# A conditional MLP with layer norm on one core: bias rows and two residual tiles ahead of the second x, GpSimd's last weight pairs over two batches, the last tile in halves

## The chip, the cores and the metric

The kernel runs on one core of a Trainium2 chip. The metric is the device time of one execution in microseconds (us), the median of the runs shown; lower is better. A core has TensorE (PE, matrix products), VectorE (DVE), ScalarE (ACT), GpSimd (POOL) and SyncE (SP), which here issues nearly all DMAs. Each engine runs its own instruction stream in order, and they wait for each other through semaphores.

## The reference

`x` is 16 batches of 512 rows by 512 columns, all fp32. An integer per batch picks one of three networks, whose output is added to `x`; the sum is normalized per row:

```python
out_nr  = gelu(x @ w1_nr  + b1_nr)  @ w2_nr  + b2_nr
out_tsr = gelu(x @ w1_tsr + b1_tsr) @ w2_tsr + b2_tsr
out_sr  = gelu(gelu(x @ w1_sr + b1_sr) @ w2_sr + b2_sr) @ w3_sr + b3_sr   # hidden 1024
out = where(c == 0, out_nr, where(c == 1, out_tsr, where(c == 2, out_sr, 0)))
y = x + out
return (y - mean(y)) * rsqrt(var(y) + 1e-5) * gamma + beta
```

## The kernel before

**Arithmetic.** Each fp32 operand is split in two parts of type fp32r, a high one and the rest (`w_hi`/`w_lo`, `x_hi`/`x_lo`, `g_hi`/`g_lo`), and a product is three matmuls: hi·hi, hi·lo, lo·hi. An NR or TSR batch is 96 matmuls of 128x512 (48 for layer 1, 48 for the last layer), an SR batch is 240. In these inputs batch 0 is NR, batch 1 is SR, batches 2 to 6 are NR. Weights are loaded once and stay in SBUF; they are split at the start: DVE and ACT split the NR weights, POOL all others, in pairs of chunks (`split_hi`, then `split_lo`; 128x1024 each). SR's pairs carry the semaphores `s_split["sr1"]`, `["sr2"]`, `["sr3"]`, TSR's four pairs `["tsr"]`.

**One batch.** PE makes the hidden layer in PSUM banks; ACT applies gelu twice per chunk (`g_hi`, and the full value in the bank); DVE makes `g_lo`; PE's last layer puts four row tiles of 128x512 in banks 4 to 7. Meanwhile SP loads the residual rows of `x` in `y`, and POOL adds the last layer's bias row to each tile (`add_bias`, semaphore `s_xb`). DVE adds the tile to the bank (`residual`), takes mean and variance (`stats`, `moments`), two tiles at a time, and makes `(y - mean) * gamma` (`centre`). POOL makes the reciprocal deviations (`deviations`, `rstd`), ACT scales by them, POOL adds beta (`shift`), SP stores the tile and reloads its place with the next batch's rows. All this tail of a batch lies beside the next batch's layer 1.

**What sets the order.** Each engine's program is written out by hand. On ACT the four scalings of a batch stand ahead of the next batch's gelus, so a late `rstd` makes the next gelu late, and then `g_lo`, and then PE. POOL's deviations stand behind whatever POOL was given in that batch. SP's queue at the start is: first x and weights in pieces, other NR weights, the two pairs `POOL_FIRST`, the five bias, gamma and beta rows in one broadcast (1280 KB), the two halves of the second x, the four residual tiles of batch 0, the other weights. Its hardware queue serves them nearly in that order.

**GpSimd's start.** POOL splits both `POOL_FIRST` pairs (sr1 0 and 1), waits for the rows, adds the biases of batch 0, and then works through the SR pairs between the deviations of batch 0 (`first`, the NR branch). The four TSR pairs come after batch 1's biases, ahead of batch 1's deviations.

**Start and end of PE.** PE runs 9 warm-up matmuls of 128x512 and 14 of 128x128 in bf16 on constants while the first data lands. In the last batch tiles 0 to 2 go the usual way; tile 3 is finished by DVE (`finish`: times rstd plus beta in one instruction) and stored by SP.

Of the kernel before, what the change touches and what calls it, by code (L numbers as in the profile page):

```python
# [37 lines left out]
FINISHED_BY_OTHERS_END = 3  # L38


N_WARM, N_WARM_SHORT = 9, 14


def conditional_mlp(nc, x, x_t, cond, weights, bias_cols, rows, out):
# [3 lines left out]
    with ctx:  # L48
# [3 lines left out]
        def sem(name):  # L52
            return ctx.enter_context(nc.semaphore(name))
# [25 lines left out]
        ones = nc.const_aps.tensor(1.0, [P, 512], mybir.dt.bfloat16)  # L79
        x_hi32 = x_hi[:, :, :].bitcast(fp32)  # L80
# [4 lines left out]
        s_rows = sem("s_rows")  # L85
# [26 lines left out]
        s_fin, s_fin_end = sem("s_fin"), sem("s_fin_end")  # L112
# [47 lines left out]

        block = ctx.enter_context(nc.Block())

        @block.sync
        def _(eng):
# [36 lines left out]
            for t in range(TT):  # L201
                load_row(0, t)
# [198 lines left out]
        def _(eng):  # L401
# [48 lines left out]
            batch(eng, cond_of, NBATCH - 1, lambda kind, read_next: body(kind, read_next, True))  # L450

        @block.vector
        def _(eng):
# [36 lines left out]
            def finish(kind, t):  # L490
# [30 lines left out]
            def body_end(kind, read_next):  # L521
# [21 lines left out]
                finish(kind, 3)  # L543
# [31 lines left out]
        def _(eng):  # L575
# [14 lines left out]
            def add_bias(kind):  # L590
                for t in range(TT):
# [141 lines left out]
```

## Time and profile before

| | |
|---|---|
| median of 3 runs | 561.88 us (561.12 to 562.71) |
| the profiled execution's own time | 561.57 us |
| its span, first to last instruction | 559.8 us |
| mean granted TensorE clock | 0.998 |
| PE busy | 549.4 us (98%) |
| DVE, ACT, POOL busy | 267.7, 213.1, 254.6 us |
| moved by DMA | 61.27 MB, mean 109 GB/s |

The span is what the trace covers; 1.8 us of the execution lie outside of it. PE's busy time contains the warm-up matmuls, and ends of matmuls are modelled, so PE's losses are read from the starts of its instructions rather than from the busy share.

### The profile page before, as it was taken

The page shows a single profiled execution, that of the slowest core. Times are in us where ns is not written, and L with a number is a line of the kernel's source. Part 1 is how long each engine was busy: PE and PEld are TensorE (multiplying, and loading weights), DVE is VectorE, ACT ScalarE, POOL GpSimd, SP SyncE. Part 2 cuts the span into 40 slices and gives each one's busy share as a digit, 9 for nine tenths or more (in the row PEclk, how much of TensorE's full clock was granted, in tenths as well). Part 3 has the DMA queues.
Part 4 walks back from the last instruction along what each step waited for, and adds up shares of the span by engine and source line. Part 5 has one row for each costly group of instructions (what it writes and reads, how often), then busy time and mean ns, then how long its engine had stood idle before and what let it go on. Part 6 is the DMA issues. An engine that isn't in the chain of part 4 may idle for free. (4 is left out here: it accounts for less than half of the span.)

```text
span 559.8 us, 8281 instructions
## 1 busy us (share of the span) xinstructions
PE 549.4 (98%) x2423; PEld 452.4 (81%) x2424; DVE 267.7 (48%) x417; ACT 213.1 (38%) x328; POOL 254.6 (45%) x225
## 2 busy tenths in 40 slices
PE   9999999999999999999999999999999999999994
PEld 6878887888888888888888888888888888888883
DVE  5661174865955856113610468212866105501656
ACT  5451335254253454214421452424255124513351
POOL 0879998575675576300430046700175300430056
PEclk9999999999999999999999999999999999999999
DMA  8875404444353443300330034400144200410032
GB/s 304 337 250 184 152 6 143 154 150 154 111 185 140 160 150 119 106 0 0 116 108 0 0 144 156 150 0 0 75 150 148 77 0 28 146 51 0 0 134 92
DMA packets 26225, 61.27 MB, mean 109 GB/s; under 512 B 3042, under 2 KB 3042, under 8 KB 26082
## 3 DMA queue, kind: packets, MB, share of 16 engines
q1 hardware_dynamic: 26208, 61.10, 31.2%
q8 instruction: 6, 0.10, 0.1%
q14 instruction: 9, 0.07, 0.0%
q10 hardware_dynamic: 2, 0.00, 0.0%
HBM read 44.31 MB, written 16.78 MB: 109 GB/s over the span
## 5 line engine op out<-in xcount | busy, mean ns | idle before, releaser
L456 DVE TENSOR_TENSOR g_lo<-bank,g_hi 128x512 fp32r<-128x512 f32 x112 | 77.4, 691 | 252.8 <-DVEq L117 252.8
L406 ACT ACTIVATE g_hi<-bank,bcol 128x512 fp32r<-128x512 f32 x112 | 77.8, 694 | 161.4 <-ACTq L117 160.2
L596 POOL TENSOR_TENSOR y<-y,row 128x512 f32<-128x512 f32 x64 | 95.2, 1507 | 51.0 <-POOLq L117 50.6
L600 POOL TENSOR_SCALAR var_eps<-mv 128x2 f32<-128x2 f32 x30 | 6.5, 218 | 227.6 <-POOLq L117 227.5
L428 ACT ACTIVATE y<-y,rstd 128x512 f32<-128x512 f32 x63 | 42.2, 717 | 172.0 <-ACTq L117 172.0
L236 PE MATMUL bank<-w_hi,g_hi 128*128 128x512 f32 x256 | 99.8, 390 | 1.2 <-PEq L117 1.2
L238 PE MATMUL bank<-w_hi,g_lo 128*128 128x512 f32 x256 | 99.7, 389 | 0.0
L237 PE MATMUL bank<-w_lo,g_hi 128*128 128x512 f32 x256 | 99.7, 389 | 0.0
L236 PE MATMUL bank<-x_hi,w_hi 128*128 128x512 f32 x240 | 93.5, 390 | 0.0
L237 PE MATMUL bank<-x_lo,w_hi 128*128 128x512 f32 x240 | 93.4, 389 | 0.0
L238 PE MATMUL bank<-x_hi,w_lo 128*128 128x512 f32 x240 | 93.4, 389 | 0.0
L610 POOL TENSOR_TENSOR y<-y,row 128x512 f32<-128x512 f32 x63 | 79.4, 1292 | 0.0
L236 PE MATMUL bank<-g_hi,w_hi 128*128 128x512 f32 x192 | 74.8, 390 | 0.8 <-issue 0.8
L238 PE MATMUL bank<-g_hi,w_lo 128*128 128x512 f32 x192 | 74.8, 389 | 0.0
L237 PE MATMUL bank<-g_lo,w_hi 128*128 128x512 f32 x192 | 74.7, 389 | 0.0
L407 ACT ACTIVATE bank<-bank,bcol 128x512 f32<-128x512 f32 x112 | 74.2, 663 | 0.0
L236 PEld LDWEIGHTS bank<-w_hi,g_hi 128*128 128x128 f32 x256 | 48.1, 188 | 11.6 <-issue 1.6
L238 PEld LDWEIGHTS bank<-w_hi,g_lo 128*128 128x128 f32 x256 | 48.1, 188 | 10.0
L237 PEld LDWEIGHTS bank<-w_lo,g_hi 128*128 128x128 f32 x256 | 48.1, 188 | 9.9
L236 PEld LDWEIGHTS bank<-x_hi,w_hi 128*128 128x128 f32 x240 | 45.1, 188 | 9.5 <-POOL w_lo L584 0.2
L238 PEld LDWEIGHTS bank<-x_hi,w_lo 128*128 128x128 f32 x240 | 45.1, 188 | 9.3
L237 PEld LDWEIGHTS bank<-x_lo,w_hi 128*128 128x128 f32 x240 | 45.1, 188 | 9.3
(42 smaller groups left out, 597.2 us busy)
## 6 DMA issues: line engine op xcount, KB each, us to landing
y<-x SPq DMA_DIRECT2D x64, 256.0 KB, 3.6
out<-y SPq DMA_DIRECT2D x64, 256.0 KB, 2.5
stage<-x_t SPq DMA_DIRECT2D x31, 512.0 KB, 3.3
w_raw<-weights SPq DMA_DIRECT2D x17, 512.0 KB, 4.7
row<-rows SPq DMA_DIRECT2D x1, 1280.0 KB, 11.4
stage<-x_t SPq DMA_DIRECT2D x2, 256.0 KB, 3.8
w_raw<-weights SPq DMA_DIRECT2D x2, 256.0 KB, 4.2
cond_sb<-cond ACTq DMA_DIRECT2D x1, 0.1 KB
```

Source lines behind the costliest of these rows:

```text
L236: eng.matmul(dst, a_hi, b_hi, start=first, stop=False)
L237: eng.matmul(dst, a_hi, b_lo, start=False, stop=False)
L238: return eng.matmul(dst, a_lo, b_hi, start=False, stop=final)
L406: eng.activation(g_hi[:, slot, :], psum, ACT.Gelu, bias=b)
L407: eng.activation(psum, psum, ACT.Gelu, bias=b).then_inc(s_g, 1)
L428: eng.activation(y[:, t, :], y[:, t, :], ACT.Copy, scale=rstd[:, t:t + 1]).then_inc(s_n, 1)
L456: eng.tensor_tensor(g_lo[:, slot, :], psum, g_hi32[:, slot, :], ALU.subtract).then_inc(s_gs, 1)
L596: eng.tensor_tensor(y[:, t, :], y[:, t, :], row[:, kind, :], ALU.add).then_inc(s_xb, 1)
L600: eng.tensor_scalar(var_eps[:, t:t + n], mv[:, t:t + n, 1], EPS, None, ALU.add).then_inc(s_var, n)
L610: eng.tensor_tensor(y[:, t, :], y[:, t, :], row[:, R_BETA, :], ALU.add).then_inc(s_fin, 1)
```

## The change

Six edits:

- SP loads the three bias rows (768 KB) and residual tiles 0 and 1 of batch 0, then the two halves of the second x, then gamma and beta (512 KB), then tiles 2 and 3.
- POOL splits only pair sr1 0 ahead of batch 0. For an NR batch 0 it then adds the biases of tiles 0 and 1, splits sr1 1, adds the biases of tiles 2 and 3, and waits for gamma and beta.
- POOL's four TSR pairs (these inputs: batch 0 isn't TSR, batch 1 isn't either): two after batch 1's biases, two after batch 2's.
- PE's warm-up is 9 long bf16 matmuls, 4 of 128x256 in fp32r, 5 short bf16 ones.
- The last tile's `finish` is two instructions of 128x256.
- Its first half is stored by SP, its second by ACT.

```diff
-N_WARM, N_WARM_SHORT = 9, 14
+N_WARM, N_WARM_HALF, N_WARM_SHORT = 9, 4, 5
...
-            eng.dma_start(row[:, :, :].rearrange("p r h -> p (r h)"), rows.rearrange("r h -> (r h)").partition_broadcast(P)
-                          ).then_inc(s_rows, 16)
+            load_rows(0, R_GAMMA, s_biases)
+            load_row(0, 0)
+            load_row(0, 1)
             for f in range(2):
                 take(eng, s_stage[f])
                 load_x(x_halves[2 + f], f)
-            for t in range(TT):
-                load_row(0, t)
+            load_rows(R_GAMMA, N_ROW, s_rows)
+            load_row(0, 2)
+            load_row(0, 3)
...
+            take(eng, s_fin_end[0])
+            eng.dma_start(out_end[0], y_end[0]).then_inc(s_out[TT - 1], 16)
...
             for _ in range(N_WARM):
                 eng.matmul(bank[7][:, :], ones[:, 0:P], ones, start=True, stop=True)
+            for _ in range(N_WARM_HALF):
+                eng.matmul(bank[7][:, 0:2 * P], ones32[:, 0:P], ones32, start=True, stop=True)
...
+            take(eng, s_fin_end[1])
+            eng.dma_start(out_end[1], y_end[1]).then_inc(s_out[TT - 1], 16)
...
-                eng.scalar_tensor_tensor(out=y[:, t, :], in0=y[:, t, :], scalar=rstd[:, t:t + 1], in1=row[:, R_BETA, :],
-                                         op0=ALU.mult, op1=ALU.add).then_inc(s_fin_end, 1)
+                for h in range(2):
+                    eng.scalar_tensor_tensor(out=y_end[h], in0=y_end[h], scalar=rstd[:, t:t + 1], in1=row[:, R_BETA, halves[h]],
+                                             op0=ALU.mult, op1=ALU.add).then_inc(s_fin_end[h], 1)
...
-            for item in POOL_FIRST:
-                split(item)
-            eng.wait_ge(s_rows, 16)
+            split(POOL_FIRST[0])
...
-                add_bias(kind)
+                if kind == NR:
+                    add_bias(kind, (0, 1))
+                split(POOL_FIRST[1])
+                add_bias(kind, (2, 3) if kind == NR else range(TT))
+                eng.wait_ge(s_rows, 16)
...
             batch(eng, cond_of, 1, bias)
             with eng.If_cmp(cond_of_0, TSR, "IS_NE"):
-                for item in POOL_TSR:
-                    split(item)
-            with eng.Fori(2, NBATCH - 1) as b:
+                split(POOL_TSR[0])
+                split(POOL_TSR[1])
+                with eng.If_cmp(cond_of_1, TSR, "IS_EQ"):
+                    split(POOL_TSR[2])
+                    split(POOL_TSR[3])
+            deviations_of_all()
+            shift_all()
+            batch(eng, cond_of, 2, bias)
+            with eng.If_cmp(cond_of_0, TSR, "IS_NE"):
+                with eng.If_cmp(cond_of_1, TSR, "IS_NE"):
+                    split(POOL_TSR[2])
+                    split(POOL_TSR[3])
+            with eng.Fori(3, NBATCH - 1) as b:
```

GpSimd at the start of the program, before: both first pairs are split, then come the loads of the condition and the four bias additions of batch 0 (`y<-y,row` at L596), and the deviations.

```order
L579 TENSOR_SCALAR w_hi<-w_raw 128x1024
L584 TENSOR_TENSOR w_lo<-w_raw,w_hi 128x1024
L579 TENSOR_SCALAR w_hi<-w_raw 128x1024
L584 TENSOR_TENSOR w_lo<-w_raw,w_hi 128x1024
L136 TENSOR_LOAD cond_sb
L634 TENSOR_LOAD cond_sb
L120 COMPARE_AND_BRANCH
L143 TENSOR_LOAD cond_sb
L596 TENSOR_TENSOR y<-y,row 128x512 x4
L600 TENSOR_SCALAR var_eps<-mv 128x2
```

The same place of the changed program (bias additions are now at L616):

```order
L599 TENSOR_SCALAR w_hi<-w_raw 128x1024
L604 TENSOR_TENSOR w_lo<-w_raw,w_hi 128x1024
L137 TENSOR_LOAD cond_sb
L652 TENSOR_LOAD cond_sb
L653 TENSOR_LOAD cond_sb
L121 COMPARE_AND_BRANCH
L144 TENSOR_LOAD cond_sb
L616 TENSOR_TENSOR y<-y,row 128x512 x2
L599 TENSOR_SCALAR w_hi<-w_raw 128x1024
L604 TENSOR_TENSOR w_lo<-w_raw,w_hi 128x1024
L616 TENSOR_TENSOR y<-y,row 128x512 x2
L620 TENSOR_SCALAR var_eps<-mv 128x2
```

Two bias additions moved ahead of the second pair, and the second pair stands between them and the other two.

GpSimd between batch 1's biases and its deviations, before (all four TSR pairs, then deviations and shift at L610):

```order
L670 COMPARE_AND_BRANCH
L579 TENSOR_SCALAR w_hi<-w_raw 128x1024
L584 TENSOR_TENSOR w_lo<-w_raw,w_hi 128x1024
L579 TENSOR_SCALAR w_hi<-w_raw 128x1024
L584 TENSOR_TENSOR w_lo<-w_raw,w_hi 128x1024
L579 TENSOR_SCALAR w_hi<-w_raw 128x1024
L584 TENSOR_TENSOR w_lo<-w_raw,w_hi 128x1024
L579 TENSOR_SCALAR w_hi<-w_raw 128x1024
L584 TENSOR_TENSOR w_lo<-w_raw,w_hi 128x1024
```

In the changed program the last two pairs have this place behind batch 2's biases, ahead of batch 2's deviations:

```order
L704 COMPARE_AND_BRANCH
L705 COMPARE_AND_BRANCH
L599 TENSOR_SCALAR w_hi<-w_raw 128x1024
L604 TENSOR_TENSOR w_lo<-w_raw,w_hi 128x1024
L599 TENSOR_SCALAR w_hi<-w_raw 128x1024
L604 TENSOR_TENSOR w_lo<-w_raw,w_hi 128x1024
L705 UNCONDITIONAL_BRANCH
L708 UNCONDITIONAL_BRANCH
L620 TENSOR_SCALAR var_eps<-mv 128x2
```

Batch 1's deviations now wait behind two pairs, and batch 2's behind the other two.

## Rows read from the trace of the kernel before

**Rows 1.** The page's first part: busy us, share of the span, instructions.

```profile
PE 549.4 (98%) x2423; PEld 452.4 (81%) x2424; DVE 267.7 (48%) x417; ACT 213.1 (38%) x328; POOL 254.6 (45%) x225
```

**Rows 2.** Windows: length, busy of PE, PEld, DVE, ACT, POOL, clock, DMA share, GB/s.

```profile
38.05:39.05 1.00, 0.16 (x2) 0.03 (x1) 0.69 (x1) 1.00 (x3) 0.82 (x2) 1.00 0.92 311
82.76:106.08 23.32, 22.08 (x97) 17.94 (x96) 14.70 (x23) 9.06 (x14) 18.63 (x17) 1.00 0.40 135
93.65:95.05 1.40, 0.16 (x2) 0.03 (x1) 0.69 (x1) 1.40 (x4) 1.40 (x3) 1.00 0.61 231
106.08:127.84 21.76, 21.76 (x97) 18.03 (x96) 15.44 (x23) 9.30 (x14) 14.08 (x14) 1.00 0.42 145
552.20:559.80 7.60, 0.12 (x1) 0.00 (x0) 3.86 (x8) 0.72 (x1) 3.81 (x5) 0.84 0.37 138
```

**Rows 3.** Timeline of PE: start us, us, instruction, idle before it.

```profile
39.05 0.47 PE L236 MATMUL bank<-g_hi,w_hi 128*128 128x512 f32 x1 [0.84 <-issue]
```

**Rows 4.** Timeline of POOL in the first 36 us.

```profile
13.90 1.81 POOL L579 TENSOR_SCALAR w_hi<-w_raw 128x1024 fp32r<-128x1024 f32 x1 [13.02 <-DMA w_raw<-weights]
...
19.50 2.40 POOL L584 TENSOR_TENSOR w_lo<-w_raw,w_hi 128x1024 fp32r<-128x1024 f32 x1 [0.18 <-POOLq L117]
23.01 6.01 POOL L596 TENSOR_TENSOR y<-y,row 128x512 f32<-128x512 f32 x4 [1.10 <-POOLq L117]
...
33.73 0.22 POOL L600 TENSOR_SCALAR var_eps<-mv 128x2 f32<-128x2 f32 x1 [2.13 <-POOLq L117]
```

**Rows 5.** Timeline of DVE, 20 to 39 us.

```profile
20.68 3.44 DVE L461 TENSOR_TENSOR x_lo<-stage,x_hi 128x1024 fp32r<-128x1024 f32 x2 [1.36 <-DVEq L117]
...
26.78 0.70 DVE L471 TENSOR_TENSOR bank<-bank,y 128x512 f32<-128x512 f32 x1 [0.56 <-DVEq L117]
...
30.58 1.29 DVE L471 TENSOR_TENSOR bank<-bank,y 128x512 f32<-128x512 f32 x2
...
38.26 0.69 DVE L456 TENSOR_TENSOR g_lo<-bank,g_hi 128x512 fp32r<-128x512 f32 x1 [3.22 <-DVEq L117]
```

**Rows 6.** Timeline of ACT: the first gelu of batch 2 and of batch 3.

```profile
92.74 0.67 ACT L406 ACTIVATE g_hi<-bank,bcol 128x512 fp32r<-128x512 f32 x1
...
114.30 0.69 ACT L406 ACTIVATE g_hi<-bank,bcol 128x512 fp32r<-128x512 f32 x1 [1.40 <-ACTq L117]
```

**Rows 7.** DMA: the rows, and tile 0 (issued at 11.93): KB, us to landing.

```profile
row<-rows SPq DMA_DIRECT2D x1, 1280.0 KB, 11.4
...
y<-x SPq DMA_DIRECT2D x1, 256.0 KB, 10.9
```

**Rows 8.** Timeline of POOL, batches 1 to 3.

```profile
76.39 2.03 POOL L579 TENSOR_SCALAR w_hi<-w_raw 128x1024 fp32r<-128x1024 f32 x1
78.61 3.14 POOL L584 TENSOR_TENSOR w_lo<-w_raw,w_hi 128x1024 fp32r<-128x1024 f32 x1 [0.18 <-POOLq L117]
81.72 1.04 POOL L579 TENSOR_SCALAR w_hi<-w_raw 128x1024 fp32r<-128x1024 f32 x1
...
89.05 0.22 POOL L600 TENSOR_SCALAR var_eps<-mv 128x2 f32<-128x2 f32 x1
...
111.41 5.05 POOL L610 TENSOR_TENSOR y<-y,row 128x512 f32<-128x512 f32 x4
...
119.65 7.00 POOL L596 TENSOR_TENSOR y<-y,row 128x512 f32<-128x512 f32 x4 [3.19 <-POOLq L117]
```

**Rows 9.** Timeline, 4.4 to 5.5 us: end of the warm-up, first weights.

```profile
4.50 0.99 PE L366 MATMUL bank<-const-bfloat16-1.0 128*128 128x128 bf16 x14
...
4.68 0.43 DVE L559 CAST w_hi<-w_raw 128x512 fp32r<-128x512 f32 x1 [3.77 <-DMA w_raw<-weights]
...
5.26 0.19 PEld L273 LDWEIGHTS bank<-x_hi,w_hi 128*128 128x128 f32 x1
```

**Rows 10.** DVE's last instruction; the last store (issued at 557.1), us to landing.

```profile
556.23 0.75 DVE L493 SCALAR_TENSOR_TENSOR y<-y,rstd,row 128x512 f32<-128x512 f32 x1 [0.44 <-DVEq L117]
...
DMA to landing us min/median/max: 2.4/2.4/2.4
```

More of the change, by code:

```diff
@@ L35 @@
 ORDER_SR = [(j, t) for j in range(2) for t in range(TT)] + [(j, t) for t in range(TT) for j in (2, 3)]
-FINISHED_BY_OTHERS_END = 3
-N_WARM, N_WARM_SHORT = 9, 14
+FINISHED_BY_OTHERS_END = TT - 1
+N_WARM, N_WARM_HALF, N_WARM_SHORT = 9, 4, 5
 def conditional_mlp(nc, x, x_t, cond, weights, bias_cols, rows, out):
@@ L79, in conditional_mlp @@
         ones = nc.const_aps.tensor(1.0, [P, 512], mybir.dt.bfloat16)
+        ones32 = nc.const_aps.tensor(1.0, [P, 256], fp32).bitcast(fp32r)
         x_hi32 = x_hi[:, :, :].bitcast(fp32)
@@ L84, in conditional_mlp @@
         s_const = sem("s_const")
-        s_rows = sem("s_rows")
+        s_biases, s_rows = sem("s_biases"), sem("s_rows")
         s_power = sem("s_power")
@@ L111, in conditional_mlp @@
         s_n = sem("s_n")
-        s_fin, s_fin_end = sem("s_fin"), sem("s_fin_end")
+        s_fin, s_fin_end = sem("s_fin"), [sem(f"s_fin_end{h}") for h in range(2)]
         s_out = [sem(f"s_out{t}") for t in range(TT)]
@@ L159, in pair @@
             return slice(first, first + 2)
+        halves = [slice(0, H // 2), slice(H // 2, H)]
+        out_end = [out.rearrange("b (p c) h -> b p c h", c=TT)[NBATCH - 1, :, TT - 1, h] for h in halves]
+        y_end = [y[:, TT - 1, h] for h in halves]
         block = ctx.enter_context(nc.Block())
@@ L175, in tile_of, with store @@
                 return dram[bass.ds(b, 1), :, t, :].rearrange("a p h -> p (a h)")
-            def store(b, t, finished=s_fin):
-                take(eng, finished)
+            def store(b, t):
+                take(eng, s_fin)
                 eng.dma_start(tile_of(out_rows, b, t), y[:, t, :]).then_inc(s_out[t], 16)
@@ L182, in load_row, with load_rows @@
                 eng.dma_start(y[:, t, :], tile_of(x_rows, b, t)).then_inc(s_row[t], 16)
+            def load_rows(first, end, landed):
+                eng.dma_start(row[:, first:end, :].rearrange("p r h -> p (r h)"),
+                              rows[first:end, :].rearrange("r h -> (r h)").partition_broadcast(P)).then_inc(landed, 16)
             def load_x(half, f):
@@ L227, in _ @@
             step(NBATCH - 1, True)
+            for t in range(TT - 1):
+                store(NBATCH - 1, t)
+            take(eng, s_fin_end[0])
+            eng.dma_start(out_end[0], y_end[0]).then_inc(s_out[TT - 1], 16)
             for t in range(TT):
-                store(NBATCH - 1, t, s_fin if t < FINISHED_BY_OTHERS_END else s_fin_end)
-            for t in range(TT):
-                take(eng, s_out[t], 16)
+                take(eng, s_out[t], 32 if t == TT - 1 else 16)
         @block.tensor
@@ L488, in variance, with finish @@
                 eng.tensor_scalar(var_eps[:, t:t + 1], mv[:, t:t + 1, 1], EPS, None, ALU.add).then_inc(s_var, 1)
-            def finish(kind, t):
+            def finish(t):
                 take(eng, s_v_end)
                 take(eng, s_rstd_end)
-                eng.scalar_tensor_tensor(out=y[:, t, :], in0=y[:, t, :], scalar=rstd[:, t:t + 1], in1=row[:, R_BETA, :],
-                                         op0=ALU.mult, op1=ALU.add).then_inc(s_fin_end, 1)
+                for h in range(2):
+                    eng.scalar_tensor_tensor(out=y_end[h], in0=y_end[h], scalar=rstd[:, t:t + 1], in1=row[:, R_BETA, halves[h]],
+                                             op0=ALU.mult, op1=ALU.add).then_inc(s_fin_end[h], 1)
             def hidden(kind):
@@ L542, in body_end @@
                 centre(kind, 3, s_v_end)
-                finish(kind, 3)
+                finish(TT - 1)
             eng.memset(cond_sb[0:1, NBATCH:NBATCH + 1], 0).then_inc(s_pad, 1)
@@ L588, in split, with add_bias @@
                 split_lo(item)
-            def add_bias(kind):
-                for t in range(TT):
+            def add_bias(kind, tiles=range(TT)):
+                for t in tiles:
                     take(eng, s_row[t], 16)
@@ L628, in _ @@
             eng.wait_ge(s_power, 1)
-            for item in POOL_FIRST:
-                split(item)
-            eng.wait_ge(s_rows, 16)
+            split(POOL_FIRST[0])
             cond_of = first_condition(eng)
-            cond_of_0 = eng.alloc_register("first_condition_Pool")
+            cond_of_0, cond_of_1 = eng.alloc_register("condition_of_0_Pool"), eng.alloc_register("condition_of_1_Pool")
             eng.reg_load(cond_of_0, cond_sb[0:1, 0:1])
+            eng.reg_load(cond_of_1, cond_sb[0:1, 1:2])
+            eng.wait_ge(s_biases, 16)
             def first(kind, read_next):
                 read_next()
-                add_bias(kind)
+                if kind == NR:
[3 more added lines that the diff above has]
+                eng.wait_ge(s_rows, 16)
                 if kind == NR:
```

## The prediction

> **What bounds the kernel now.** I read the page's busy times first: PE is busy for 549.4 of 559.8 us, no other engine for half of the span [rows 1]. So only three things can change the time: how long until the first real matmul, the places where PE stands, and what follows its last one. The busy share hides them, so I went through PE's starts. An undisturbed NR batch is 96 matmuls in 21.76 us [rows 2], 0.2267 us each. Starts farther apart occur at two places. The first matmul of batch 1's second layer starts at 39.05 and was due at 38.05 [rows 2, 3]. Batch 2 takes 23.32 us, 1.56 more than batch 3, and 1.40 of it lie before its last layer, due at 93.65 [rows 2]; the other 0.16 are lost by the matmuls around the stop, and I count as much for the first stop. Ahead of the first real matmul lie 5.3 us, behind the last 7.6 [rows 2, 9]. The removable waits are 1.2 + 1.56 = 2.75 us, 0.5% of the time.
>
> **Stall 1, at 38.05.** PE starts 0.1 behind the end of `g_lo` (38.26 + 0.69 = 38.95) [rows 3, 5]. `g_lo` waits for gelu, gelu for the scalings of batch 0, those for POOL's second deviations at 33.73 [rows 4], those for DVE's chain, and that for POOL's biases: they start at 23.01 after 1.10 idle [rows 4], when tile 0 has landed (11.93 + 10.9 = 22.83) [rows 7], and DVE adds the second tile at 26.78, after having stood 0.56 for it, and the third at 30.58 [rows 5].
>
> Now biases and tiles 0 and 1 come first. They are 768 + 512 = 1280 KB, as much as the five rows were, so tile 1 lands where these did, at 6.75 + 11.4 = 18.15 [rows 7] (the issue is the row load's of before), tile 0 earlier, and the second x as before. POOL is free of pair sr1 0 at 13.90 + 1.81 + 0.18 + 2.40 = 18.3 [rows 4]. It adds two tiles by 20.9 (1.3 each), and the conditions' loads, one more than before, are issued while it splits. DVE is then held by its x split, to 24.12, or 24.5 with more of GpSimd's work beside it [rows 5]. Two additions 0.6 apart put the second at 24.7 to 25.1 instead of 26.78: 1.7 to 2.1 earlier. Tile 2 must follow 3.8 later (30.58 - 26.78), at 28.9. POOL splits sr1 1 from 20.9; beside the x split a pair has cost 2.03 + 0.18 + 3.14 = 5.35 [rows 8], so until 26.3, then tile 2's bias until 27.6 and tile 3's until 28.9: in time. Gamma and beta take the place at which tiles 0 and 1 stood, so about 22 to 23.5, in time too. So the deviations of 33.73 come at 32.0, `g_lo` is there at 37.3, and PE goes on at 38.05. The stall needs 1.0 of the 1.7: it is gone, **-1.2** (bounds -1.3 and 0). The next pair in need, sr2 0, ends 1.7 earlier too.
>
> **What the split pair costs.** Batch 1 needs sr1 1 at 27.17 (5.3 + 96 matmuls). Before it was there at 21.9 [rows 4]. Now it is there at 24.5 (uncontended: 1.05 + 0.18 + 2.4) or 26.3 (contended): hidden, with 0.9 to spare. If tile 0 landed late, each us beyond these 0.9 would cost one.
>
> The contended pair is where a rule speaks against the change. The Trainium skill, GPSIMD Engine Reference, Specifications, says that GpSimd shares its SBUF interfaces with VectorE and contends with DVE instructions that have two SBUF inputs. The x split is one, and the trace agrees: 2.03 and 3.14 beside it against 1.04 and 2.41 beside instructions that read a PSUM bank. If the rule held for every DVE instruction beside POOL, the pair would still end at 26.3 and the sum would not move; it narrows the cover from 2.7 to 0.9.
>
> **Stall 2, at 93.65.** POOL's four TSR pairs end at 89; deviations start at 89.05, 6.29 behind the batch's start [rows 8]. ACT's four scalings follow and the first gelu is at 92.74, 3.69 behind; in batch 3 it is at 114.30, 8.22 behind its start, and there ACT stood 1.40 before it, so only the matmuls set it [rows 6]. So: PE goes on 6.0 us behind the first deviations D of the previous batch, and its last layer is due 10.88 behind the batch's start S. Stall = D - S - 4.88; with 6.29 it gives 1.41, and the trace has 1.40. With two pairs only, batch 1's deviations are on time (POOL is free some 7.3 us earlier) and batch 2 has no stall.
>
> But the other two pairs go to batch 2's tail, whose POOL time isn't free. Undisturbed, shift starts about 5.5 behind a batch's start (111.41 - 106.08 = 5.33), and the biases end 15.24 behind that (119.65 + 7.00 - 111.41) [rows 8]: 20.7. Batch 3's deviations in fact wait for just these biases. Two uncontended pairs are 2 x 3.6 = 7.2 (81.72 to 89.05 holds two beside the same DVE work) [rows 8]. D is then 28.0 behind batch 2's start, 6.2 behind batch 3's (21.76 later), and the stall 6.2 - 4.88 = 1.35: what batch 2 lost, batch 3 loses. With the shortest biases, as batch 2's own (0.8 shorter), it is 0.5; with biases 0.4 longer 1.75. I take 1.35 against 1.40: **-0.1** (bounds -1.0 and +0.3). After batch 3 POOL is late as it was after batch 2, and catches up as it did.
>
> **Warm-up.** `w_hi` is there at 5.11, the first real weight load is at 5.26, right behind the last of 14 short matmuls, which take about 0.06 each [rows 9]. Nine of these, 0.5 us, are replaced by four fp32r matmuls of 256 columns, which the trace doesn't show. Half of a 512-column one's pace is 0.11, together 0.45; a weight load of this type alone takes 0.19 [rows 9], together 0.76; the full pace of 0.2267 gives 0.9. So first data waits for nothing more (down to 5.18, -0.1) or 0.4 more. The weight load is nearest to what such a stream must do, less what overlaps: **+0.1**. It moves everything behind it one to one.
>
> **The end.** `finish` starts at 556.23 and takes 0.75; its store lands 2.4 behind the issue [rows 10]. Two halves take 0.75 at least and twice that at most; I take 0.1 more than the whole, so the second ends at 557.1. Its store moves 128 KB less: at most 0.42 (at 311 GB/s, the fastest stretch of [rows 2]), at least nothing. That ACT issues it may cost up to 0.2. So -0.4 to +0.3 with the halves as taken; I take **-0.05**.
>
> The Trainium skill, DMA: Bandwidth & Descriptors, Anatomy of one DMA, gives some 2.0 us of a transfer as fixed, whatever its size. By this an estimate for the half is 2.2 us, and the end would gain 0.1.
>
> **Sum.** 561.57 (the profiled execution: a span of 559.8 and 1.8 around it) - 1.2 - 0.1 + 0.1 - 0.05 = 560.3. It is 0.3 under the median of the runs shown; taken from 561.88 the forecast is 560.6, 0.22% less. A measurement of this kernel can tell about 0.3%, 1.7 us, from no change.
>
> **Rivals.**
>
> A. Both stalls go: batch 3 doesn't stall. For it: two pairs are half of four, and the biases of batch 2 took 0.9 less in one batch than in the next. Against it: D must come at 4.88 behind the start of batch 3, that is 1.3 us sooner than the rows give. 561.9 - 1.2 - 1.56 = 559.1. Chance 0.15.
>
> B. Nothing is gained: stall 1 stays in part because sr1 1 or a late tile holds batch 1 or DVE's chain (tile 0's last piece may be late: before, it took 2.3 us more than the 256 KB ahead of it would need), or the warm-up takes back 0.4 and the end 0.3. 561.9. Chance 0.17.
>
> C. Slower: the two pairs in batch 2's tail run contended. At 5.35 each instead of 3.6 they add 3.5 us to D, and the stall in batch 3 becomes 4.9 in place of 1.4: 561.9 - 1.2 + 3.5 = 564.2. It decides from 1.3 us of extra POOL time on (no gain), and from 3.0 on it is measurably slower. Against it: the two pairs from 81.72 on had DVE's same residual and statistics work beside them and weren't stretched. Chance 0.05.
>
> The forecast has 0.63: stall 1 gone, stall 2 moved; its own range is 559.9 to 561.4.
>
> **Chances.** Faster by over 0.3% needs less than 560.2: all of A and a quarter of the forecast, 0.31. Slower: C and a little of B, 0.06. Same: 0.63. The range reaches from A to B: 559.0 to 561.9.
>
> **What would show it.** Stall 1: POOL's first bias at about 18.4, DVE's second addition near 25, PE's starts without a step at 38. The pair: `w_lo` of sr1 1 ends by 26.5, and batch 1 starts 96 matmuls behind batch 0. Stall 2: no step in batch 2, deviations of batch 2 about 6.2 behind batch 3's start, and a step of some 1.3 there before its last layer. Warm-up: the first real weight load near 5.4. End: about 7.5 us from the last matmul to the last landing. The forecast is wrong if batch 3 has no step (A), if POOL's biases in batch 2 end sooner than 20 us behind its start, or if batch 1 starts late.

## Result and the profile after

The changed kernel takes 562.66 us, median of 17 runs (562.13 to 564.67), against 561.55 (560.97 to 562.71, 17 runs) of the kernel before on the same chip: ratio of the means 1.0027, 95% interval 1.0017 to 1.0037. That is 1.1 us slower by the medians and 1.5 by the means, which six executions near 564.4 pull up. It is less than the 0.3% named as the bound, but it is outside of the forecast's range (559.0 to 561.9) and on the other side of 561.88. The profiled execution took 562.56 us, its span is 560.8 (before: 561.57 and 559.8).

PE's starts, read as in [rows 2]: batch 0 from its first weight load, the gap ahead of batch 1, batch 1, batch 2, batch 3 up to its last layer, its stop, and the rest to the last matmul. Windows of the changed kernel, with the columns of [rows 2]:

```profile
5.21:27.26 22.05, 22.01 (x96) 17.77 (x96) 16.34 (x19) 11.83 (x17) 12.83 (x7) 1.00 0.92 354
27.26:28.76 1.50, 0.16 (x2) 0.03 (x1) 1.50 (x4) 0.00 (x0) 1.46 (x2) 1.00 0.75 213
28.76:83.24 54.48, 54.48 (x240) 45.12 (x241) 21.12 (x29) 19.12 (x30) 46.78 (x32) 1.00 0.46 151
83.24:105.04 21.80, 21.80 (x97) 17.97 (x96) 15.71 (x27) 9.29 (x14) 13.42 (x13) 1.00 0.41 145
105.04:115.92 10.88, 10.88 (x49) 8.82 (x47) 5.27 (x10) 2.69 (x5) 10.06 (x10) 1.00 0.28 96
115.92:118.02 2.10, 0.16 (x1) 0.03 (x1) 0.69 (x1) 2.10 (x5) 2.10 (x3) 1.00 0.44 166
118.02:553.40 435.38, 435.38 (x1920) 360.37 (x1920) 204.55 (x320) 165.28 (x255) 162.94 (x152) 1.00 0.25 88
```

Two stops, as before, but neither is where it was. The stop at 38.05 is gone and batch 1 starts 1.50 late instead. The stop in batch 2 is gone (21.80 for 96 matmuls and 0.04 of the next) and batch 3 has one of 2.10 instead of 1.40. Against before, batch 2 starts 0.48 later (83.24 for 82.76), batch 3's last layer 1.06 later (118.02 for 106.08 + 10.88 = 116.96), and the last matmul ends 1.2 later.

The opening, on DVE and on POOL (timelines, with the columns of [rows 4] and [rows 5]; the second row is the second of the first row's two instructions):

```profile
21.42 4.93 DVE L480 TENSOR_TENSOR x_lo<-stage,x_hi 128x1024 fp32r<-128x1024 f32 x2 [1.94 <-DVEq L118]
22.94 3.40 DVE L480 TENSOR_TENSOR x_lo<-stage,x_hi 128x1024 fp32r<-128x1024 f32 x1
26.27 1.28 DVE L490 TENSOR_TENSOR bank<-bank,y 128x512 f32<-128x512 f32 x2
30.65 1.28 DVE L490 TENSOR_TENSOR bank<-bank,y 128x512 f32<-128x512 f32 x2
38.33 0.69 DVE L475 TENSOR_TENSOR g_lo<-bank,g_hi 128x512 fp32r<-128x512 f32 x1 [3.21 <-DVEq L118]
```

```profile
18.40 2.53 POOL L616 TENSOR_TENSOR y<-y,row 128x512 f32<-128x512 f32 x2
20.90 1.05 POOL L599 TENSOR_SCALAR w_hi<-w_raw 128x1024 fp32r<-128x1024 f32 x1
22.13 3.14 POOL L604 TENSOR_TENSOR w_lo<-w_raw,w_hi 128x1024 fp32r<-128x1024 f32 x1 [0.18 <-POOLq L118]
25.23 3.49 POOL L616 TENSOR_TENSOR y<-y,row 128x512 f32<-128x512 f32 x2
33.80 0.22 POOL L620 TENSOR_SCALAR var_eps<-mv 128x2 f32<-128x2 f32 x1 [2.13 <-POOLq L118]
```

POOL's biases start at 18.40, 4.6 earlier than in [rows 4], and sr1 1 ends at 25.27. But DVE's x split runs from 21.42 to 26.35, where [rows 5] has 20.68 and 3.44: the second addition starts near 26.87 (the second of the two from 26.27), 26.78 before. `g_lo` starts at 38.33 for 38.26. All that POOL won in the opening was lost on DVE.

Batches 2 and 3 on POOL, to be held against [rows 8]:

```profile
89.05 0.22 POOL L620 TENSOR_SCALAR var_eps<-mv 128x2 f32<-128x2 f32 x1 [3.26 <-POOLq L118]
90.13 5.04 POOL L630 TENSOR_TENSOR y<-y,row 128x512 f32<-128x512 f32 x4
98.40 6.20 POOL L616 TENSOR_TENSOR y<-y,row 128x512 f32<-128x512 f32 x4 [3.23 <-POOLq L118]
104.69 1.05 POOL L599 TENSOR_SCALAR w_hi<-w_raw 128x1024 fp32r<-128x1024 f32 x1
109.52 2.40 POOL L604 TENSOR_TENSOR w_lo<-w_raw,w_hi 128x1024 fp32r<-128x1024 f32 x1 [0.18 <-POOLq L118]
112.00 0.22 POOL L620 TENSOR_SCALAR var_eps<-mv 128x2 f32<-128x2 f32 x1
```

The biases end at 104.60, the two pairs take 7.2, the first deviations start at D = 112.00, 6.96 behind batch 3's start: 6.96 - 4.88 = 2.08, and the stop is 2.10.

Warm-up and end, on PE, PEld, DVE and in the DMA issues (the rows for [rows 9, 10]):

```profile
4.11 0.80 PE L381 MATMUL bank<-const-float32-1.0 128*128 128x256 f32 x4
4.75 0.46 PE L383 MATMUL bank<-const-bfloat16-1.0 128*128 128x128 bf16 x5
```

```profile
5.21 0.76 PEld L288 LDWEIGHTS bank<-x_hi,w_hi 128*128 128x128 f32 x4 [0.18 <-issue]
```

```profile
557.42 0.88 DVE L513 SCALAR_TENSOR_TENSOR y<-y,rstd,row 128x256 f32<-128x256 f32 x2 [0.43 <-DVEq L118]
```

```profile
out<-y SPq DMA_DIRECT2D x2, 256.0 KB, 2.5
out<-y SPq DMA_DIRECT2D x1, 128.0 KB, 1.9
out<-y ACTq DMA_DIRECT2D x1, 128.0 KB, 2.1
```

The first real weight load is at 5.21 (5.26 before). From one matmul's pace (0.2267) behind the last matmul's start to the end of the span it is 7.44 us (7.64 before).

**The late batch 1.** No engine's data were late at 27.26: sr1 1 was there at 25.27 and the x split at 26.35. What stands in the trace is PE's own branch at the end of batch 0's step. Its instruction (line, count, ns as min/median/max, start), of the changed kernel, then of before:

```profile
L398 PEldq COMPARE_BRANCH  x1: 3668/3668/3668, 23.2 to 23.2; - x1
```

```profile
L381 PEldq COMPARE_BRANCH  x1: 449/449/449, 23.1 to 23.1; - x1
```

Beside it the DMA queues of 24.2 to 25.0 in the changed kernel and of 20.2 to 21.0 in before (queue: packets, MB, share):

```profile
q8 instruction: 1, 0.02, 8.0%
```

```profile
q8 instruction: 1, 0.02, 8.2%
```

Each is one fetch of 16 KB of instructions. Read in slices of 0.1 us, it begins at 20.5 in before, 2.6 us ahead of the branch; in the changed kernel it begins at 24.2, 1.0 behind the branch's start, and the branch ends 2.7 us later, at 26.9. PE's program before the branch had grown shorter by five matmuls and their weight loads.

### The profile page after: what moved, and what is told of

It is laid out like the page before. It is cut to its first block and busy times, and to the rows that moved or that the text cites. A ratio compares the mean times of both kernels' runs of the same rounds, so it can differ in the third digit from the quotient of the medians.

```text
span 560.8 us, 8275 instructions
## 1 busy us (share of the span) xinstructions
PE 549.4 (98%) x2418; PEld 452.2 (81%) x2419; DVE 269.8 (48%) x418; ACT 213.2 (38%) x328; POOL 253.7 (45%) x225
## 5 line engine op out<-in xcount | busy, mean ns | idle before, releaser
L616 POOL TENSOR_TENSOR y<-y,row 128x512 f32<-128x512 f32 x64 | 94.7, 1500 | 49.5 <-POOLq L118 49.3
L480 DVE TENSOR_TENSOR x_lo<-stage,x_hi 128x1024 fp32r<-128x1024 f32 x30 | 50.6, 1726 | 5.8 <-DVEq L118 5.8
```

The source lines that it names most:

```text
L480: eng.tensor_tensor(x_lo[:, c, :], stage[:, f, :, :], x_hi32[:, c, :], ALU.subtract).then_inc(done, n)
```

## Experiments

The kernel before is the base where nothing else is said. Times are medians with their range and count; kernels of one group ran on one chip, beside the same runs of before; a ratio is that of the means, this kernel's to before's. "Gap" is a step in PE's starts beyond 0.2267 us a matmul; of the steps in the first 10 us, which are waits for first data, only e6's is listed (the others are up to 0.3 in the tables' kernels).

**First group: each part alone** (before 561.87, 33 runs). Two theories: P, batch 1 is late through PE's own program; T, through the opening's DMA traffic.

```
e1:  N_WARM, N_WARM_HALF, N_WARM_SHORT = 9, 4, 5      # and its loop
e2:  load_rows(0, R_GAMMA), load_row(0, 0..1), second x, load_rows(R_GAMMA, N_ROW), load_row(0, 2..3)
     bias 0, 1; split(POOL_FIRST[1]); bias 2, 3
e3:  two pairs behind batch 1, two behind batch 2
e4:  last tile finished and stored in halves
```

> The kernel before with the changed warm-up alone (9 long, 4 fp32r of 256 columns, 5 short matmuls). Theory P (placement): ten instructions fewer ahead of PE's loop move its code, and the branch that ends batch 0 must fetch its target from memory. Then PE's branch at the end of batch 0 takes 3.7 us here as in the changed kernel, batch 1 starts 1.5 us late, the stall at 38 us is gone in exchange (1.2), and the time is 0.3 to 0.4 us above before's. Theory T (traffic): that fetch is late because of the new order of the opening loads. Then the branch takes 0.45 us here, all stalls are those of before, and the time is within 0.1 us of before's.

> The kernel before with the new opening alone (bias rows and two tiles ahead of the second x, gamma and beta behind it, pair sr1 1 between the biases). Theory T (traffic): the branch at the end of batch 0 takes 3.7 us, batch 1 starts 1.5 us late, no stall at 38: 0.4 us above before. Theory P (placement): the branch takes 0.45 us, batch 1 starts on time, and since DVE's x split ends at 26.3 as in the changed kernel, DVE's chain is as late as before and the stall at 38 stays at 1.0 to 1.2: within 0.2 us of before.

> The kernel before with GpSimd's four last pairs spread over two batches alone. The stall ahead of batch 2's last layer (1.4 us) goes, one ahead of batch 3's last layer comes. If its size follows from when batch 1's tail ends, and that was late in the changed kernel by DVE's x split beside GpSimd's two pairs (5.45 us for two instructions), it is 2.1 us here too and the time 0.5 to 0.7 us above before's. If the changed kernel's 2.1 came from its opening, it is 1.3 to 1.5 here and the time is the same as before's.

> The kernel before with the last tile finished and stored in halves alone. From the last matmul to the end the changed kernel takes 7.4 us, before took 7.6: expected 0.2 us less than before, too little to be told in the time, visible in the trace. A rival: the second queue costs as much as the half saves, nothing.

| alone | us | ratio, 95% | branch ns | gaps |
|---|---|---|---|---|
| e1 warm-up | 561.84 (560.95 to 562.18, 11) | 0.9988 to 1.0006 | 3650 | 1.48 at 27.8, 0.98 at 94.6 |
| e2 opening | 561.79 (561.42 to 562.03, 11) | 0.9990 to 1.0009 | 433 | 0.92 at 38.2, 1.41 at 93.8 |
| e3 pairs 2, 2 | 562.24 (561.28 to 562.65, 11) | 0.9993 to 1.0011 | 1003 | 0.87 at 38.3, 1.67 at 115.6 |
| e4 halves | 561.54 (561.18 to 561.83, 11) | 0.9986 to 1.0004 | 443 | 0.08 at 39.1, 1.43 at 93.5 |

Windows of the two gaps of e1:

```profile
27.77:29.25 1.48, 0.17 (x2) 0.03 (x1) 1.48 (x4) 0.00 (x0) 1.48 (x2) 1.00 0.70 191
94.63:95.61 0.98, 0.16 (x2) 0.03 (x1) 0.69 (x1) 0.98 (x3) 0.98 (x2) 1.00 0.45 167
```

P is right on the cause and T is refuted: the warm-up alone makes the branch late, the opening alone doesn't. P's 0.3 to 0.4 us in the time did not come, since the stop in batch 2 fell to 0.98. No part alone costs or brings anything measurable, so the loss is in their combination. The stop of e3, 1.67, lies between the two sizes that its theories gave (2.1, and 1.3 to 1.5), so it decides for neither. The branch of e3, 1003 ns, is longer than in before too; PE doesn't stop for it. e2 also refutes my term for stall 1; its DVE rows:

```profile
21.36 4.99 DVE L467 TENSOR_TENSOR x_lo<-stage,x_hi 128x1024 fp32r<-128x1024 f32 x2 [1.90 <-DVEq L117]
26.28 1.28 DVE L477 TENSOR_TENSOR bank<-bank,y 128x512 f32<-128x512 f32 x2
```

In e4 the stop at 38 nearly vanished without a cause of its own: its first real matmul came at 6.07 instead of 5.3, and PE went on at 39.2 nonetheless. Where a stop waits for another engine's chain, a late start in front of it costs nothing.

**Second group: what makes the branch late, and a way without the stop** (before 561.90, 32 runs).

```
e5:  changed kernel, N_WARM, N_WARM_SHORT = 9, 14        # before's warm-up
e6:  before,         N_WARM, N_WARM_SHORT = 9, 9         # five fewer, no other type
e7:  changed kernel, N_WARM_SHORT = 10                   # 23 warm-ups again, four of them fp32r
e8:  e5 with the last four pairs as 2, 1, 1 behind batches 1, 2 and 3
```

> The changed kernel with the warm-up of before (9 long and 14 short bf16 matmuls). Theory I (the loss needs the new warm-up: late branch, and behind it a later start of DVE's and GpSimd's work in batch 1's tail): the branch takes 0.45 us, batch 1 is on time, the stall at 38 stays near 0.9 and the one in batch 3 is 1.7 as with the spread alone; 561.6 to 562.0 and no run above 563. Rival (the opening and the spread interact by themselves): the stall in batch 3 is 2.1 and some runs are above 564 here too.

> The kernel before with 9 short warm-up matmuls in place of 14: nothing of another type, only ten PE instructions and 0.3 us fewer ahead of the loop. If their number decides whether the branch that ends batch 0 finds its target, it takes 3.65 us and batch 1 starts 1.5 us late, as with the new warm-up. If the fp32r type or its length decides, it takes 0.45 us.

> The changed kernel with 10 short matmuls in place of 5, behind the four of fp32r: as many PE instructions ahead of the loop as in the kernel before. If the number decides, the branch takes 0.45 us, batch 1 is on time, the runs above 564 are gone, and the time is 0.5 to 1.0 us under the changed kernel's 562.66; the longer warm-up takes up to 0.3 of it back. If the type decides, all is as in the changed kernel.

> The changed kernel with the warm-up of before and the four last pairs as two, one, one behind the biases of batches 1, 2 and 3. One pair takes 3.6 us, so the deviations come 24.5 us behind the start of batch 2 or 3, 2.7 behind the next batch's start, and the formula (that minus 4.88) is below zero: no stall in batches 2, 3 and 4. 1.5 to 1.8 us less than with two and two: 560.1 to 560.4. If the stall in batch 3 isn't made by the pairs, it stays.

| | us | ratio, 95% | branch ns | gaps |
|---|---|---|---|---|
| e5 | 562.05 (561.45 to 562.41, 11) | 0.9992 to 1.0010 | 433 | 0.97 at 38.7, 1.66 at 116.1 |
| e6 | 561.82 (561.21 to 562.30, 10) | 0.9987 to 1.0006 | 2808 | 0.59 at 8.2, 0.64 at 28.1, 1.39 at 94.4 |
| e7 | 562.15 (561.68 to 562.48, 11) | 0.9995 to 1.0013 | 443 | 0.93 at 38.5, 1.93 at 115.9 |
| e8 | 560.38 (560.05 to 561.12, 10) | 0.9964 to 0.9983 | 443 | 0.92 at 38.4, none behind |

The times forecast for e7 and e8 came; e5's is 0.05 above its range. The branch rows of e6 and e7:

```profile
L381 PEldq COMPARE_BRANCH  x1: 2808/2808/2808, 24.0 to 24.0; - x1
```

```profile
L398 PEldq COMPARE_BRANCH  x1: 443/443/443, 23.6 to 23.6; - x1
```

Five bf16 matmuls less make the branch late (e6, 2.8 us for the expected 3.65, and a stop of 0.64 only, as PE had already lost 0.59 in batch 0), the fp32r matmuls with five bf16 ones put back don't (e7): it is the number of PE's instructions (18 or 23 warm-up matmuls; no other number was run), not their type. And the stop in batch 3 is that of two pairs in one batch: e8 differs from e5 in this alone, takes 1.7 us less, and the stop is gone, as the formula D - S - 4.88 wants it (e8's POOL):

```profile
104.26 1.05 POOL L595 TENSOR_SCALAR w_hi<-w_raw 128x1024 fp32r<-128x1024 f32 x1
105.50 2.39 POOL L600 TENSOR_TENSOR w_lo<-w_raw,w_hi 128x1024 fp32r<-128x1024 f32 x1 [0.18 <-POOLq L117]
107.98 0.22 POOL L616 TENSOR_SCALAR var_eps<-mv 128x2 f32<-128x2 f32 x1
```

**Third group: the opening, and the branch once more** (before 561.76, 23 runs).

```
e9:   e8 with before's opening
e10:  e8, the new loads, but POOL splits both first pairs ahead of the four biases
e11:  e6, and PE waits for the first piece of w_hi behind its warm-up
e12:  the changed kernel
```

> As the two, one, one kernel, but with the opening of before (five rows in one load, both first pairs split ahead of the biases). If the new opening gave nothing, because DVE's x split lasts longer beside GpSimd's pair by what the biases come earlier, the stall at 38 stays near 1.0 and the time is the same, 560.2 to 560.6. If it gave something after all, it is 0.5 to 1.0 us slower.

> As the two, one, one kernel with the new order of loads, but GpSimd splits both first pairs ahead of the four biases, as before. The tiles have landed by 19, so the first bias starts at 21.9 instead of 23.0, and no pair stands beside DVE's x split. If contention with the pair is what held DVE, its x split ends near 25 instead of 26.5, the second residual addition is 0.8 to 1.1 us earlier than 26.8, and the stall at 38 falls from 0.92 to 0.0 to 0.3: 559.4 to 560.0. If the later landing of the second x holds it, the stall stays above 0.6.

> The kernel before with 9 short warm-up matmuls in place of 14, and one wait of PE more, for the first weight piece (landed at 4.65 us), ahead of its loop: the branch hint of batch 0 runs at 4.5 us or later, as before, and not at 2.9; the code stays shorter by ten instructions less that wait. If the time of the hint decides, the branch takes 0.45 us. If the place of the code decides, it takes 2.8 to 3.7 us.

> The changed kernel once more, unchanged, to see its two groups of times (562.1 to 563.0 at a mean clock of 0.997, and 564.0 to 564.7 at 0.994). If the second group is TensorE's clock falling to its lower level after a stall, a trace of that group shows a stretch of some 3 us at 1.2 GHz behind one of the two stalls, and it comes in a third of the runs. If it is a longer wait for instructions, the trace shows a longer branch and the clock as before.

e9 took 560.08 us (559.78 to 560.22, 6 runs; ratio 0.9956 to 0.9980), e10 559.99 (559.50 to 560.10, 6; 0.9953 to 0.9977), so the new opening is worth nothing or costs 0.3. The 0.3 us that part e8 from these two lie outside of the span: all three profiles span 558.3 us, but e8's ten executions have 1.93 to 2.08 us outside of it, e9's and e10's twelve 1.70 to 1.80. e13, below, which has e8's opening and pairs, has 1.93 to 2.05. Why, no run shows.

e10 was to tell what holds DVE in the opening. Its x split took 4.07 us and ended at 25.61, sooner than the changed kernel's, and still the second addition isn't earlier than in before (26.78); DVE stands for POOL's bias of tile 1, which now comes late:

```profile
27.02 0.70 DVE L486 TENSOR_TENSOR bank<-bank,y 128x512 f32<-128x512 f32 x1 [0.80 <-DVEq L117]
```

So with the pair between the biases DVE's split sets the second addition (near 26.87 in the changed kernel), and with the pair ahead of them POOL's bias does (27.02). The expected 0.8 to 1.1 us did not come. The stop at 38 did fall to 0.31 in e10, but to 0.29 in e9 as well: both had their first real matmul at 6.07, e8 at 5.50, and PE goes on at 39.3 in all three. e10's time lay in the expected range by luck.

e10 is the fastest kernel of this study, 1.8 us under before. e11 took 561.80 (561.08 to 562.26, 10; 0.9989 to 1.0008) with a branch of 3731 ns and a gap of 1.57 at 28.2: PE passed the place where the branch's target is announced (the kernel's hint instruction, below; its first start is 5.9 us, for 4.4 in before and 2.9 in e6) 1.5 us later than in before, and the fetch was still late:

```profile
L380 PEldq BRANCH_PREFETCH_HINT  x2: 50/50/50, 5.9 to 29.1; - x2
```

So an early announcement isn't the cause; the length of PE's program ahead of the branch, or where its code lies, is what is left. e11 also has no stop in batch 2 (0.09 at 95.4): there PE comes so late, S = 84.55, that D = 89.20 is in time.

The late branch can be followed through all 20 profiles. The fetch begins 15.2 to 16.2 us behind the first real matmul in the nine with 23 warm-up matmuls, and 18.8 to 19.4 behind it in the eleven with 18. In these eleven and in e3 the branch ends 2.6 to 2.7 us behind the fetch's start, and in the eleven the first matmul of batch 1 starts 1.8 to 1.9 us behind the branch's end (the starts of fetch and branch are read to 0.1 us). In e3 the fetch begins at 21.7 and the branch ends at 24.4: a branch of 1003 ns, but soon enough for batch 1, which is due near 27.4.

e12 repeats the loss: 562.65 (562.05 to 564.15, 11; 1.0008 to 1.0026), branch 3936 ns, gaps 1.76 at 27.7 and 1.94 at 116.7.

**Fourth group: which parts make the loss together** (before 561.74, 27 runs).

```
e13:  changed kernel, pairs as 2, 1, 1
e14:  e1 + e3                    # warm-up and pairs; opening and end of before
e15:  e1 + e2                    # warm-up and opening; four pairs behind batch 1
e16:  the changed kernel, one execution
```

> The changed kernel with its own warm-up, its last four pairs as 2, 1, 1 behind batches 1, 2 and 3. Theory L (the late start of batch 1 costs its 1.5 us only where no later stall absorbs it): with before's warm-up this layout gave 560.4 and kept a stall of 0.9 at 38, which the late start swallows, so 560.4 + 1.5 - 0.9 = 561.0. Rival F (a late start is free): 560.4. Rival R (the warm-up costs more than its late branch, through the group of times near 564): median above 561.5.

> Before with the new warm-up and the pairs 2 and 2, opening and end as before. Theory I (the loss is the late start together with the stall in batch 3, which it doesn't shrink): gap of 1.5 at 28, none at 38, 1.7 to 2.1 at 116, sum 3.4 to 3.7 and 562.3 to 562.6. Rival O (the opening, with sr1 1 split beside DVE's x split, is needed for the loss): about 561.9, the gap in batch 3 below 1.2.

> Before with the new warm-up and the new opening, all four pairs behind batch 1. Theory I: the late start swallows the stall at 38 and shrinks the one of batch 2 to about 1.0, as with the warm-up alone: sum 2.6, 561.8. Rival O: the stall of batch 2 is 1.4 or more and the time 562.2 to 562.5.

> The changed kernel once more, one look. Three of four times it should be near 562.2, with gaps of 1.5 to 1.8 at 28 and 1.9 to 2.1 at 116. If it falls near 564.3: theory C (the clock falls to its lower level for some us during a stop of PE) wants a slice with PEclk well below 1 beside one of the stops; the rival, a longer stop, wants a step of 1.7 us more in PE's starts at full clock.

e14 took 562.98 us (562.37 to 563.53, 11; ratio 1.0022, 1.0013 to 1.0031), e15 561.88 (561.23 to 562.22, 11; 0.9992 to 1.0010). Theory I's pattern holds: warm-up and pairs together lose the 0.2%, neither does alone, and the opening and the halves aren't needed for it. e14's time lies above the 562.3 to 562.6 that I had given, its gaps sum to 3.45, as forecast. The windows of e14's two stops:

```profile
27.86:29.38 1.52, 0.16 (x2) 0.03 (x1) 1.21 (x4) 0.00 (x0) 1.00 (x2) 1.00 0.84 232
116.51:118.44 1.93, 0.16 (x1) 0.03 (x1) 0.69 (x1) 1.93 (x5) 1.93 (x3) 1.00 0.48 180
```

and POOL's first deviations D of e14, e1 and e15, one row of each:

```profile
112.42 0.22 POOL L603 TENSOR_SCALAR var_eps<-mv 128x2 f32<-128x2 f32 x1
```

```profile
89.60 0.22 POOL L603 TENSOR_SCALAR var_eps<-mv 128x2 f32<-128x2 f32 x1
```

```profile
89.38 0.22 POOL L609 TENSOR_SCALAR var_eps<-mv 128x2 f32<-128x2 f32 x1
```

S is the stop's due time less 10.88 (the batch whose last layer waits):

| | branch | S | D | D - S - 4.88 | stop |
|---|---|---|---|---|---|
| before, four pairs in batch 1 | in time | 82.76 | 89.05 | 1.41 | 1.40 |
| e1, four pairs | late | 83.75 | 89.60 | 0.97 | 0.98 |
| e15, four pairs | late | 83.15 | 89.38 | 1.35 | 1.34 |
| e3, two and two | in time | 104.70 | 111.22 | 1.64 | 1.67 |
| e14, two and two | late | 105.63 | 112.42 | 1.91 | 1.93 |
| changed kernel | late | 105.04 | 112.00 | 2.08 | 2.10 |

With four pairs in a row D is the end of POOL's own work, which doesn't ask when PE started: the later S, the smaller the stop. With two and two, D hangs on batch 2's deviations, shift and biases, all of them behind PE: from e3 to e14 S moves by 0.93 and D by 1.20. There the late branch stops being free: the stop behind it doesn't shrink by what PE lost, as e1's did. That it grew, from 1.67 to 1.93, isn't the late start's doing alone, as e18 below shows. e5 and e7, two and two with the branch in time, have 1.66 and 1.93. e13 took 560.65 (560.47 to 561.63, 11; ratio 0.9984, 0.9975 to 0.9993), with one gap of 1.43 at 27.4 and none behind. Against e8's ratio of 0.9973 that is 0.6 us more, which is L's figure (a stop of 1.5 in place of one of 0.9). But the two intervals overlap, e8 ran on another chip, and the median lies between F's 560.4 and L's 561.0: R is refuted, and L rests on the gaps, 1.43 in place of 0.92, more than on the time.

Two more executions of the changed kernel:

> The changed kernel, one look, for a profile of one of the times near 564.3. If it is one: theory C (the granted clock falls behind one of PE's stops) wants a slice with PEclk well below 1 and matmuls farther apart than 0.2267 us there; the rival, a longer stop, wants a step of 1.7 us more in PE's starts at full clock. Else near 562.6 with gaps of 1.5 to 1.8 at 28 and 1.9 to 2.1 at 116.

> The same once more: near 564.3 with the marks of theory C or of its rival, or near 562.6 with gaps of 1.5 to 1.8 at 28 and 1.9 to 2.1 at 116.

The three executions took 562.99, 562.91 and 562.17 us, branches of 3868, 3716 and 3496 ns, gaps of 1.70, 1.54 and 1.32 ahead of batch 1, of 2.09, 2.12 and 1.60 in batch 3. None fell near 564.3.

They show something else, though. In the tail of batch 1 DVE's x split meets POOL's last pair of that batch. DVE's and POOL's rows there, of e16 (stop 2.09):

```profile
76.68 5.22 DVE L480 TENSOR_TENSOR x_lo<-stage,x_hi 128x1024 fp32r<-128x1024 f32 x2 [0.27 <-DVEq L118]
```

```profile
76.45 1.05 POOL L599 TENSOR_SCALAR w_hi<-w_raw 128x1024 fp32r<-128x1024 f32 x1
77.69 3.14 POOL L604 TENSOR_TENSOR w_lo<-w_raw,w_hi 128x1024 fp32r<-128x1024 f32 x1 [0.18 <-POOLq L118]
```

and the second instruction of that split:

```profile
78.50 3.41 DVE L480 TENSOR_TENSOR x_lo<-stage,x_hi 128x1024 fp32r<-128x1024 f32 x1
```

Then of e18, the same kernel (stop 1.60), with its split's second instruction:

```profile
76.37 3.24 DVE L480 TENSOR_TENSOR x_lo<-stage,x_hi 128x1024 fp32r<-128x1024 f32 x2 [0.27 <-DVEq L118]
77.56 2.05 DVE L480 TENSOR_TENSOR x_lo<-stage,x_hi 128x1024 fp32r<-128x1024 f32 x1
```

```profile
76.52 2.02 POOL L599 TENSOR_SCALAR w_hi<-w_raw 128x1024 fp32r<-128x1024 f32 x1
78.72 3.14 POOL L604 TENSOR_TENSOR w_lo<-w_raw,w_hi 128x1024 fp32r<-128x1024 f32 x1 [0.18 <-POOLq L118]
```

Of two of these instructions that overlap, the one that starts first keeps the time it takes alone (1.2 us for an instruction of the split, 1.05 for `w_hi`, 2.4 for `w_lo`), and the other ends about its own time behind the first one's end. In e16 `w_lo` waits for the split's first instruction, to 78.57, and ends at 80.83; the split's second, begun at 78.50, waits for all of `w_lo` and ends at 81.91. In e18 DVE is ahead by 0.15 us: the split's second instruction waits only for `w_hi`, to 78.54, ends at 79.61, and `w_lo` waits for it.

So the first meeting decides whether DVE waits for POOL's 1.05 or for its 2.4. In the 20 profiles of this case, at this place, the split takes 3.2 to 3.9 us in all, its second instruction 2.05 to 2.07, and `w_hi` 2.0 to 2.1 wherever DVE was first (14). The split takes 4.6 to 5.5, its second instruction 3.41 or 3.42, and `w_hi` 1.05 where POOL was first or level (6: the changed kernel, e11, e12, e14, e16, e17). `w_lo` takes 3.1 to 3.3 in all 20. All six are among the eleven with the late branch; their DVE splits start at 76.15 to 77.23, those of the nine with the branch in time at 75.56 to 76.35, and POOL doesn't start later for it.

## Why the prediction was wrong, step by step

**Stall 1, forecast -1.2.** The failed step is "DVE is then held by its x split, to 24.12, or 24.5 with more of GpSimd's work beside it". It was held to 26.35 (in e2 too), for two reasons. The split started 0.74 later, because the second x landed later than "as before": ACT's `x_hi`, its first user, starts at 20.21 for 19.49. Part of this is the spread between executions, since the split starts anywhere from 20.45 to 21.73 in the eight profiles with before's loads, and from 21.21 to 21.89 in the twelve with the new ones. And it took 4.93 us for 3.44, which is the larger part. Beside sr1 1's pair it took 4.8 to 5.5 in all eleven profiles with the new order of POOL, always with the pair's first half at 1.05 and the split's second instruction, which waits for `w_lo`, at 3.40 to 3.42. I had priced the contention on POOL's side (5.35 for the pair, where it took 4.37) and left DVE 0.4 for it. The 3.44 that I built on is also the shortest of all: there POOL stood idle for tile 0 from 21.9 to 23.01 [rows 4], so the split's second instruction, at 22.91, was ahead of the bias and took 1.21; in the seven other profiles with before's opening the bias was ahead, that instruction took 2.3 and the split 4.4 to 4.6. That the biases start at 18.4 and that sr1 1 ends by 26.3 was right, and worth nothing. In e2 the stop stays at 0.92: rival B, "stall 1 stays in part because sr1 1 or a late tile holds batch 1 or DVE's chain", is what the opening does by itself. In the changed kernel the stop at 38 is absent only because PE comes there late.

**A term that was missing: batch 1 starts late, +1.58 (1.50 and 0.08 at the restart), of which stall 1's 1.16 was given back.** The prediction costed the warm-up as PE's time alone. e1, e6, e7 and e11 show that fewer instructions ahead of PE's first branch make its target's 16 KB come too late. The prediction named "if batch 1 starts late" as a sign of error, but for another cause, a late sr1 1, and priced only that (1 us per us). 0.42 are left; batch 2's start is 0.48 later.

**Stall 2, forecast -0.1.** The mechanism was right, moved as said to batch 3, with the formula right to 0.03 in every row of the table, and the two pairs uncontended at 7.2. The term was mis-sized: 2.10 in place of 1.35. "shift starts about 5.5 behind a batch's start" measured 6.9 (90.13 - 83.24), and the biases end 21.4 behind it for 20.7. In front of them is again DVE's x split beside POOL's pair: 5.45 us from 76.15 in the changed kernel, where before's split, ahead of the stretched `w_hi` of [rows 8], took 3.82. Stops with the short split are 1.60 to 1.67 (e3, e5, e18) and 1.93 (e7), with the long one 1.93 to 2.12 (e12, e14, e16, e17, the changed kernel): the order of those two instructions is worth some 0.3 to 0.5 by the changed kernel's own profiles (1.60 against 1.94 to 2.12), and e7 shows that it isn't all. Even without it the term would have been 1.6 and not 1.35. Rival C's mechanism (contended pairs in batch 2) did not occur, nor did its 564.2; that the time went up, as C has it, is no point for it.

**Warm-up's own time, forecast +0.1:** the first real weight load moved by -0.05, to 5.21, with `w_hi` there at 5.10. In e1, with the same warm-up, it is at 5.34. The four fp32r matmuls take 0.64 us to the next start here (4.11 to 4.75, 0.16 each), 0.84 in e1 and 1.03 in e14, so the term is no larger than the spread between executions. **The end, forecast -0.05:** -0.2 by the profiles, the halves taking 0.88 for 0.75 and the half's landing 1.9 to 2.1 for 2.4. In the twelve profiles with the halves it is 7.4 to 7.5 us behind the last matmul, in the eight without 7.6 to 8.0. The estimate of 2.2 us for the half, which the prediction made with a figure of the Trainium skill (DMA: Bandwidth & Descriptors, Anatomy of one DMA), is too long: the trace has 1.9 on SP's queue and 2.1 on ACT's. That section's figure is for DMAs issued from GpSimd, which these aren't. e4's median doesn't tell the gain from nothing.

**Sum by the profiles:** batch 2's start +0.48, then +0.58 more to batch 3's last layer, some 0.1 of small steps behind it, -0.2 at the end: +1.0 us of span, as measured. That the medians say 1.1 agrees.

**Open.** Seven of the 31 times of the changed kernel (17, e12's 11, the three single ones) lie between 564.05 and 564.67 us at a mean granted clock of 0.994, all others at or below 563.2 with 0.995 to 0.998. No other kernel had such a time. No profile of one was caught, so where these 1.7 us go isn't shown. Without them the first comparison's median is 562.49, still 0.9 above before. Also open: why e8 and e13 have 0.25 us more than the others outside of their spans, and what exactly about the length of PE's program decides when the fetch goes out.

## What to carry to other kernels

Before taking an instruction away from the engine that bounds the kernel, look at how long its branches take before and after: an edit of five dummy matmuls moved a 0.45 us branch to 2.8 to 3.9 us. A stop that ends when another engine's own chain of work does swallows delays in front of it, and one that hangs on the bounding engine's last batch hands them on, so two edits that each measure as nothing can lose together; test the pairs, not only the parts. When work is pulled forward on POOL, price what DVE's work beside it becomes, not only what POOL's does, and spread background work one item per batch (e8 to e10: 1.5 to 1.8 us less than before here) rather than two.

## What the runs showed of the hardware

- A branch of PE whose target isn't there: 2808 to 3936 ns in the eleven profiles with 18 warm-up matmuls, 433 to 449 in eight with 23, and 1003 in e3. In the late ones the 16 KB fetch on the instruction queue starts behind the branch, by 0.2 to 1.3 us; the branch ends 2.6 to 2.7 us behind the fetch's start.
- DVE and GpSimd beside each other, both on SBUF inputs: they take turns by whole instructions. The one that is first by as little as 0.07 us (e13: 76.28 and 76.35) keeps its pace, and the other ends its own time behind it: `w_hi` 2.0 to 2.1 us for 1.05, `w_lo` 3.1 to 3.3 for 2.4, an instruction of the x split 2.1 behind `w_hi` and 3.4 behind `w_lo` for 1.2. Where the recorded starts are equal (76.15 in the changed kernel, 76.49 in e17) or 0.02 apart (e5, 21.45 and 21.47, DVE first), DVE paid. The Trainium skill (GPSIMD Engine Reference, Specifications) has the contention for DVE instructions with two SBUF inputs, as the split's are, and the traces agree.
